# Opening of a dequantising FFN kernel: loads in order of use, tile 1 mixed earlier, first quarter of tile 0 in one piece

## The reference

```python
W = weights[condition]                       # (64, 64, 64)
y = einsum('bct,bcd->bdt', x, W)             # the mix
p = qweight.reshape(N, groups, 3)            # qweight: (1024, 768) int32
v0, v1 = p[..., 0] & 63, p[..., 0] >> 6 & 63
v2, v3 = p[..., 1] & 63, p[..., 2] & 63
w = (stack(v0, v1, v2, v3) - zero_point) * scale
out = x + einsum('bsk,nk->bsn', y, w) + bias
```

## Time and profile before

| | us |
|---|---|
| median of 3 runs | 286.94 (286.89 to 287.38) |
| profiled execution, its own time | 287.01 |
| its span, first to last instruction | 284.8 |
| TensorE busy | 278.3 (98%) |
| VectorE busy | 186.2 (65%) |
| GpSimd busy | 95.6 (34%) |
| ScalarE busy | 84.0 (29%) |

### The profile page before, as it was taken

The page is one execution under the profiler, slowest core; times in us unless marked ns, Lnnn a source line. Parts: engine busy times, 40 slices in busy tenths (PEclk is TensorE's granted clock), DMA queues, the critical chain, the costliest instruction groups (busy, mean ns, idle before and its releaser), DMA issues.

```text
span 284.8 us, 8521 instructions
## 1 busy us (share of the span) xinstructions
PE 278.3 (98%) x3323; PEld 232.8 (82%) x3323; DVE 186.2 (65%) x254; ACT 84.0 (29%) x170; POOL 95.6 (34%) x38
## 2 busy tenths in 40 slices
PE   7999999999999999999999999999999999999995
PEld 3988887788888888888888888888888888888885
DVE  3675689855567666765559555676667655595554
ACT  3678313531044310633007310343106330060000
POOL 0008753244440444304443344404443044430000
PEclk9999999999999999999999999999999999999999
DMA  7992463355114541355213551144412562101112
GB/s 277 399 304 81 160 228 111 127 174 203 74 74 154 157 155 68 124 161 202 83 74 115 163 219 74 74 152 158 150 74 98 167 208 98 74 37 74 74 74 74
DMA packets 20685, 39.48 MB, mean 139 GB/s; under 512 B 6850, under 2 KB 7106, under 8 KB 20674
## 3 DMA queue, kind: packets, MB, share of 16 engines
q1 hardware_dynamic: 19730, 36.96, 37.1%
q10 hardware_dynamic: 944, 2.38, 2.2%
HBM read 22.54 MB, written 16.78 MB: 138 GB/s over the span
## 4 chain that ended last, share of the span: by engine, by line
PE 95%; DMA 1%; DVE 1%; ACT 1%; issue 1%; ACTq 1%
PE o_ps L283 72%; PE y_ps L283 11%; PE y_ps L252 9%; DMA q_raw<-in_L_ffn_qweight_dram 1%; PE o_ps L252 1%; PE y_ps L265 1%; PE o_ps L265 0%; ACT y_hi L415 0%; PE o_ps L294 0%; ACTq L142 0%; ACT L437 0%; PE y_ps L294 0%; DVE y_lo L500 0%; DVE q_int L488 0%; DVE o_sb L601 0%
## 5 line engine op out<-in xcount | busy, mean ns | idle before, releaser
L283 PE MATMUL o_ps<-qT,y_hi 128*128 128x512 f32 (+2 forms) x464 | 175.3, 382 | 0.0
L283 PE MATMUL o_ps<-qT,y_lo 128*128 128x512 f32 (+2 forms) x464 | 174.8, 381 | 0.0
L621 POOL TENSOR_TENSOR resid<-x_sb,bias_bc 128x1024 f32<-128x1024 f32 x32 | 94.9, 2969 | 155.7 <-DVE o_sb L529 135.1
L283 PEld LDWEIGHTS o_ps<-qT,y_hi 128*128 128x128 f32 x464 | 86.6, 188 | 16.9 <-ACT qT L431 0.2
L283 PEld LDWEIGHTS o_ps<-qT,y_lo 128*128 128x128 f32 x464 | 86.7, 188 | 16.8
L521 DVE TENSOR_TENSOR o_sb<-o_ps,scale_bc 128x512 f32<-128x512 f32 x54 | 37.3, 692 | 75.5 <-PE o_ps L283 75.5
L415 ACT ACTIVATE y_hi<-y_ps 128x512 fp32r<-128x512 f32 x57 | 29.8, 610 | 101.5 <-PE y_ps L252 101.3
L529 DVE TENSOR_TENSOR o_sb<-o_sb,resid 128x512 f32<-128x512 f32 x63 | 51.1, 815 | 2.1
L406 ACT ACTIVATE junk<-x_sb 128x1024 bf16<-128x1024 f32 x32 | 33.8, 1058 | 58.7 <-DMA x_sb<-in_x_dram 58.7
L510 DVE SCALAR_TENSOR_TENSOR resid<-zs_bc,ysum,resid 128x1024 f32<-128x1024 f32 x32 | 43.7, 1366 | 0.0
L500 DVE TENSOR_TENSOR y_lo<-y_ps,y_hi 128x512 fp32r<-128x512 f32 x57 | 35.7, 684 | 6.5 <-ACT y_hi L415 6.5
(11 more groups left out here) (34 smaller groups left out, 62.1 us busy)
## 6 DMA issues: line engine op xcount, KB each, us to landing
x_sb<-in_x_dram SPq DMA_DIRECT2D x32, 512.0 KB, 3.3
out_dram<-o_sb SPq DMA_DIRECT2D x63, 256.0 KB, 2.1
q_raw<-in_L_ffn_qweight_dram ACTq DMA_DIRECT2D x6, 384.0 KB, 5.4
w_sb<-in_L_cond_weights_dram SPq DMA_DIRECT2D x63, 16.0 KB, 2.0
q_raw<-in_L_ffn_qweight_dram SPq DMA_DIRECT2D x2, 384.0 KB, 6.9
scale_bc<-_L_ffn_weight_scale_dram SPq DMA_DIRECT2D x1, 512.0 KB, 5.1
zs_bc<-n_weight_zero_point_dram SPq DMA_DIRECT2D x1, 512.0 KB, 5.8
bias_bc<-in_L_ffn_bias_dram SPq DMA_DIRECT2D x1, 512.0 KB, 6.6
```

The lines of the kernel that those rows point to most:

```text
L283: last = nc.tensor.matmul(bank, part[:, slot, kt, :], qT[:, kt, col:col + width], start=(kt == 0 and part is y_hi), stop=(kt == KT - 1 and ...
L621: nc.gpsimd.tensor_tensor(resid[:, j % RING, :], x_sb[:, j % RING, :], bias_bc[:], ALU.add).then_inc(xbias_ready, 1)
```

## The change

It has four parts. (1) Loads: ACT issues blocks 0 to 5 and both second w halves of tiles 0 and 1; SP issues x and the first w halves of tiles 0 and 1, picks four indices, then waits until block 3 has landed, and only then issues blocks 6 and 7 and all the rest in the old order. (2) TensorE mixes tile 1 right after transposing block 2. (3) Columns 0 to 255 of tile 0 are computed in one piece of 16 matmuls of 256 columns, its `y_hi` part ahead of the transposes of block 3 and its `y_lo` part behind; before, they were two pieces of 16 matmuls of 128 columns. (4) Columns 256 to 511 of tile 0 go to another PSUM bank, and VectorE's and ScalarE's orders follow.

```diff
+        second_quarter = free_banks[1][:, 2 * P:NH]
...
             load_x(1, 0)
-            load_w(1, 0)
-            for n in (4, 6):
+            load_w_half(sp, 1, 0, pick(sp, 2))
+            picked = [pick(sp, entry) for entry in range(4, 2 * RING)]
+            sp.wait_ge(q_loaded[3], 16)
+            for n in (6, 7):
                 load_q(sp, n)
             for j in range(2, RING):
                 load_x(j, 0)
-                load_w(j, 0)
+                for half in range(2):
+                    load_w_half(sp, j, half, picked[(j - 2) * 2 + half])
...
+            def first_quarter(part):
+                return products(o_ps[:, 0, 0:2 * P], 0, 2 * P, 0, parts=(part,))
...
-            pe.wait_ge(qt_ready, 1)
-            pe.wait_ge(y_hi_ready, 2)
-            products(o_ps[:, 0, 0:P], 0, P, 0, parts=(y_hi,))
-            wait_linear(0, 0, 0)
-            products(o_ps[:, 0, 0:P], 0, P, 0, parts=(y_lo,))
-            pe.wait_ge(qt_ready, 2)
-            products(o_ps[:, 0, P:2 * P], P, P, 0).then_inc(o_ps_ready[0], 1)
-            transpose_q(3)
             wait_mix(1, 0)
             mix(1, y_banks[1])
+            pe.wait_ge(qt_ready, 2)
+            pe.wait_ge(y_hi_ready, 2)
+            first_quarter(y_hi)
+            transpose_q(3)
+            pe.wait_ge(y_lo_ready, 2)
+            first_quarter(y_lo).then_inc(o_ps_ready[0], 1)
             pe.wait_ge(qt_ready, 4)
-            pe.wait_ge(left_copied, 1)
-            products(o_ps[:, 0, 2 * P:NH], 2 * P, NH - 2 * P, 0).then_inc(o_ps_ready[0], 1)
+            products(second_quarter, 2 * P, NH - 2 * P, 0).then_inc(o_ps_ready[0], 1)
             transpose_q(4)
             transpose_q(5)
-            wait_linear(1, 0, 0)
+            pe.wait_ge(left_copied, 1)
+            pe.wait_ge(y_lo_ready, 4)
...
             pe.wait_ge(qt_ready, 7)
+            pe.wait_ge(scaled[0], 1)
             pe.wait_ge(xsum_ready, RING)
...
             load_w_half(act, 0, 1, pick(act, 1))
-            for n in (2, 3, 5, 7):
+            load_q(act, 2)
+            load_w_half(act, 1, 1, pick(act, 3))
+            for n in (3, 4, 5):
                 load_q(act, n)
             place_q(0)
             high(0, 0, y_banks[0])
             place_q(1)
             place_q(2)
+            high(1, 0, y_banks[1])
+            place_q(3)
             sum_x(0, 0)
-            place_q(3)
-            high(1, 0, y_banks[1])
...
             low(0, 0, y_banks[0])
             unpack_q(3)
+            unpack_q(4)
+            low(1, 0, y_banks[1])
             dve.wait_ge(o_ps_ready[0], 1)
             nc.vector.tensor_copy(o_sb[:, 0, 0:2 * P], o_ps[:, 0, 0:2 * P]).then_inc(left_copied, 1)
-            unpack_q(4)
             unpack_q(5)
-            low(1, 0, y_banks[1])
             dve.wait_ge(o_ps_ready[0], 2)
```

More of the change, by code:

```diff
@@ L451, in _ @@
             place_q(5)
+            sum_x(2, 0)
             place_q(6)
-            sum_x(2, 0)
             sum_x(3, 0)
@@ L540, in _ @@
             unpack_q(3)
+            unpack_q(4)
+            low(1, 0, y_banks[1])
             dve.wait_ge(o_ps_ready[0], 1)
             nc.vector.tensor_copy(o_sb[:, 0, 0:2 * P], o_ps[:, 0, 0:2 * P]).then_inc(left_copied, 1)
-            unpack_q(4)
             unpack_q(5)
-            low(1, 0, y_banks[1])
             dve.wait_ge(o_ps_ready[0], 2)
-            nc.vector.tensor_copy(o_sb[:, 0, 2 * P:NH], o_ps[:, 0, 2 * P:NH]).then_inc(scaled[0], 1)
+            nc.vector.tensor_copy(o_sb[:, 0, 2 * P:NH], second_quarter).then_inc(scaled[0], 1)
             unpack_q(6)
```

## The result

The changed kernel takes 289.84 us (median of 6 runs, 289.5 to 291.3) against 286.91 us before (6 runs, 286.87 to 287.53): ratio 1.01, 95% interval 1.008 to 1.0119. It is slower by 2.9 us; the forecast was 287.0 with 287.7 as its upper end. The profiled execution took 289.86 us, with a span of 287.6. Some executions of any of these kernels run at a lower granted clock and take some per cent longer (294.18 us at 0.982 for one that takes 288.3 at 1.0); all medians and ratios here leave these out.

A forecast was written before the change was run, and what follows sets the result against it. The prediction took a chain from the bias row's landing through GpSimd and VectorE as the bound. TensorE's 1.0 us hidden and bias + 0.1 gave 287.01 + 0.1 = 287.1 profiled, 287.0 against the median; range 286.0 to 287.7.

The forecast's parts named there:

- Loads: DMA queues in the opening: the bias row's landing counts, and the hold delays it by 0.1 us, at most 0.95.
- the cover is 1.96 - 0.95 = 1.0 us against 0.95 needed: no gap: At block 3's landing: ACT's queued blocks 4 and 5 keep the DMA engines busy until block 6 starts.
- SP's issues behind the hold (11 of them at about 0.5 us, indices already picked) stay ahead of the engines: SP's queue after the wait: issuing one by one leaves no further gap for the DMA engines.
- Rival C: Opening loads: the hold delays the bias, each 0.1 us of gap costing 0.1; full price 0.95, 287.9 us; chance 0.11.
- The chain from the bias: From the bias landing at 22.04, GpSimd and VectorE block each other until `low` of tile 4 at 49.14, without TensorE.
- TensorE's 1.0 us: Opening: TensorE reaches its first full product 1.0 us earlier, 1.58 - 0.1 - 0.3 - 0.2, bounds 0.2 to 1.5.
- The spared 1.58: Tile 0's first quarter in one piece: 2.03 us in place of 3.61 on TensorE, less 0.1 for the cut.
- The 1.0 us is gone: it costs nothing and wins nothing: Head of the loop: TensorE's gain is lost waiting for VectorE, so the time doesn't move.
- the wait for `y_lo`: Ahead of the fourth mix of group 1: TensorE's idle time grows from 0.58 to about 1.6 us.
- rival A: TensorE's gain comes through because the VectorE and GpSimd chain gives way: 285.9 us, at best 285.4; chance 0.13.

The follow-up runs named there:

- e13: Changed kernel, hold kept, with the scale, zero and bias rows issued by GpSimd once block 3 is in: 289.56 us.
- e3: Changed kernel, hold kept, with the bias row issued ahead of scale and zero point: 289.89 us.
- experiment 6: GpSimd held after its first four additions until VectorE finishes group 0: changed kernel 287.79 us, changed kernel without hold 286.17, kernel before 287.17.
- e8: Changed kernel with SP's wait put on block 2 in place of block 3, so that it never bites: 286.21 us.
- e1: Changed kernel without SP's wait for block 3: 286.18 us.
- e2, e12: Label not tied to a run in the text given, so neither its change nor its time can be assigned.
- e4: Changed kernel without the hold and with the bias row issued ahead of scale and zero point: 286.78 us.
- e5: Kernel before, with only the bias row issued ahead of scale and zero point: 287.89 us.
- e6: Changed kernel, hold kept, with GpSimd waiting before its fifth addition until VectorE has finished group 0: 287.79 us.
- e9: Changed kernel without the hold, with GpSimd waiting before its fifth addition until VectorE has finished group 0: 286.17 us.
- e10: Kernel before, with only GpSimd waiting before its fifth addition until VectorE has finished group 0: 287.17 us.
- e14: Changed kernel without the hold, with the scale, zero and bias rows issued by GpSimd after block 5: 286.98 us.
- e7: Changed kernel with SP held until block 5 in place of block 3: 291.09 us.
- e11: Label not tied to a run in the text; TensorE's program of before, which fits the kernel before with only the hold (288.31 us, repeated 289.07).

## Why the prediction was wrong, step by step

**The step that failed** stands under *Loads*: "the cover is 1.96 - 0.95 = 1.0 us against 0.95 needed: no gap", and behind it "SP's issues behind the hold (11 of them at about 0.5 us, indices already picked) stay ahead of the engines". I took 0.1 us for it, and 0.95 as the most; it measured 3.88. First, there was no cover. I had reckoned that blocks 4 and 5 follow block 3 one after the other, with 1.96 us of transfer still to do when it is reported. In fact all but 0.1 MB of them had moved by then, and they were reported at 11.93 and 12.89, behind block 3 at 10.99. So the engines ran all but dry (0.10 MB in all from 11 to 12 us). Second, the restart came late: SyncE left the hold at 11.01; I had no row for block 3's landing in the new order, and reckoned with the 9.85 at which its unpacking began in the old one. Without the hold SyncE begins the same list at 7.86, and before at 6.83, and has a lead over the engines that covers it. Third, the gap isn't the first issue's alone: from 12 to 15 us the engines move only 255, 191 and 227 GB/s, against 402 when full.

Why they come back so slowly stays open. It isn't shown to be SyncE's rate of issuing. Between 11.01 and 16.46 it issues 2 x 384 KB of weights, 2 x 512 KB of x and 64 KB in four halves of w: 1,856 KB in 5.45 us, or 340 GB/s. Without the hold it needs 5.17 us for the same list (7.86 to 13.03), hardly less. By 13.2 it had issued 1,280 KB, and by 15 the engines had moved only 0.66 MB of its queue. And a second issuer (e13) didn't fill them either. With the hold on block 5 the engines stand still from 12 to 13 us and then move 252, 353 and 304 GB/s.

**Rival C** named the mechanism ("everything behind the wait is late together"), and between the changed kernel and the one before its rule held: 3.88 us at the bias are 3.71 at the fourth mix. It isn't a rule for any bias (e3: 3.44 earlier at the bias, 1.30 at the fourth mix). Its price of 0.95, for the first issue's gap alone, was the mis-sized term. I gave it a chance of 0.11, since I held the cover for two blocks.

**The chain from the bias** to `low` of tile 4, by way of GpSimd and VectorE, was right, to 0.2 us in 27. Holding GpSimd back (experiment 6) shows that GpSimd is the cause: `residual` 1.27 instead of 3.10. That one blocks the other, and doesn't merely slow it, rests on the 1.08 us between GpSimd's end and VectorE's. The Trainium skill, "SBUF — State Buffer", section "SBUF: two separate sides", has this rule (the one that starts first holds the port for its whole instruction), and these runs agree. What the chain lacked is that the scale and zero rows sit in it too (e3).

**TensorE's 1.0 us.** It measured 0.61 (transposes of block 4) with the hold, and 0.27 at the head of the loop in e8. The spared 1.58 was less 0.39: the split piece takes 1.22 + 1.20 = 2.42, not 2.03, where I took off 0.1. The first mix came 0.2 later (6.84 for 6.64), w of tile 1 cost 0.16 (forecast 0.3), block 3 cost 0.25, or 0.78 without the hold, which I had not put down at all.

**"The 1.0 us is gone: it costs nothing and wins nothing"** was right for the wait for `y_lo`: e8 and e1 reach the fourth mix at 49.96 and 50.16, before at 49.97. And yet e8 is 0.8 us faster than before: its first product behind that mix starts at 51.33, against 52.03. The wait for `y_lo` was not the last one there. Before, TensorE was held up once more inside the fourth mix, until 51.01, and this stop doesn't move with `y_lo`: in the ten profiles that have it (before, e2, e4, e5, e6, e9, e10, e12, e13, e14) it ends 4.6 to 5.1 us behind the start of the group's three mixes. So a TensorE that comes earlier to that place does gain. I had seen the interruption of 0.47 and taken it for none of the change's business; without the hold, rival A would have been partly right.

**What stays open** is TensorE's stop without a semaphore. In the opening it leaves 33 matmuls of the mix in the changed kernel, e6 and e7, and 50 in e11, e10 and e5 (TensorE's program of before); in the fourth mix it falls at one and the same matmul of TensorE's program in all ten profiles that have it. So the place is the program's; whether there is a stop is not: e10 and e5 have no hold and stop, and the fastest run of e3, with the hold, doesn't. The DMA records of the traces show a packet of 16 KB of the kind "instruction" ahead of each stop:

| kernel | packet, from to | TensorE goes on | after the packet's end |
|---|---|---|---|
| changed | 23.34 to 24.28 | 25.67 | 1.39 |
| e7 | 23.22 to 24.17 | 25.62 | 1.45 |
| e11 | 22.82 to 23.76 | 25.15 | 1.39 |
| before, fourth mix | 48.38 to 49.55 | 51.01 | 1.46 |
| e9, fourth mix | 48.11 to 49.12 | 50.48 | 1.36 |

In e8, which has no stop in the opening, that packet runs from 20.42 to 21.68. At all 16 stops in the profiles TensorE goes on 1.1 to 1.5 us after the end of such a packet. That fits a TensorE that waits for its own instructions. No run here moved the instructions alone, so it is argued and not shown, and why that packet came 2.9 us later in the changed kernel than in e8 is not known (in e3, with the hold, it came at 19.29).

## What to carry to other kernels

A queue held back for the sake of the first transfers makes everything behind it late, and here by somewhat more than the hold: SyncE went on 3.15 us later and the bias was usable 3.71 us later. Transfers that are still queued elsewhere are a cover only for the bytes that they have not moved yet when the wait ends; here that was 0.1 MB of two blocks. Ask what is last in that queue and what hangs on it. If the last transfer starts a chain without slack, order the queue, and don't hold it: here the order alone (with the hold on block 2, which never bites, 286.21 us) is 0.24% faster than before (0.13% to 0.35%) and 3.6 us faster than with the hold; the same kernel with no hold at all (e1) has an interval that includes no change. When an engine's wait is taken away, look at the next few microseconds of the same engine before counting the gain.

## What the runs showed of the hardware that was not expected

Issuing a DMA of 16 KB takes SyncE as long as one of 512 KB: half of a w 0.48 us (5.12), two of them 1.14 with the step between, the row `bias_bc` 0.45. The bias took 8.3 us from issue to landing with the DMA engines moving 220 GB/s from 19 to 21 us, against 6.6 before with 317. DMA engines that have run dry can stay low for some 3 us although more than they move has been issued (191 to 255 GB/s from 12 to 15 us, in the changed kernel). When a load is reported, those behind it in the same queue can be all but done: blocks 4 and 5, issued at 5.95 and 6.43 behind block 3 (5.32), had moved all but 0.1 of their 0.79 MB when block 3 was reported at 10.99. And TensorE can stop for 0.4 to 4.1 us inside a run of matmuls with no semaphore to wait for, at a place that the program sets; these were all in the first 57 us.
